# Row maxima of attention scores: two maxima per VectorE instruction, with cells and PSUM banks ordered for it

## The reference, cut to what matters

```python
xn = layer_norm(x, norm_w, norm_b)
q = (xn @ q_w + q_b).reshape(Bx, Tx, H, -1)
k = (xn @ k_w + k_b).reshape(Bx, Tx, H, -1)
att = jnp.einsum('bnhl,bmhl->bnmh', q, k)
att = att + (1.0 - mask) * -1000000.0
att = jax.nn.softmax(att, axis=2)
v = ((xn @ v_w + v_b) * src_mask[:, :, None]).reshape(Bx, Tx, H, -1)
y = jnp.einsum('bnmh,bmhl->bnhl', att, v).reshape(Bx, Tx, Dx)
...
h = layer_norm(y, sb_norm_w, sb_norm_b) * (1.0 + scale) + shift
h = jax.nn.silu(h) @ out_w + out_b
return x + h
```

## Time and profile before

| | us |
|---|---|
| median of three runs | 611.57 |
| lowest and highest | 608.18, 619.8 |
| the profiled execution's own time | 609.58 |
| its span in the trace | 607.4 |
| PE busy in it | 560.7 (92%) |
| DVE busy | 447.2 (74%) |
| ACT busy | 337.8 (56%) |
| POOL busy | 104.3 (17%) |

### The profile page before, as it was taken

How to read it: one execution, slowest core, us unless ns; L and a number is a source line. 1 busy time by engine, 2 the same in 40 slices (tenths; PEclk the granted TensorE clock), 3 DMA queues, 4 the chain that set the end, 5 groups by cost and what they waited for, 6 DMA issues and landing times. The chain is left out here.

```text
span 607.4 us, 8411 instructions
## 1 busy us (share of the span) xinstructions
PE 560.7 (92%) x3060; PEld 274.5 (45%) x3060; DVE 447.2 (74%) x896; ACT 337.8 (56%) x411; POOL 104.3 (17%) x171
## 2 busy tenths in 40 slices
PE   8998996999999899999989999999889999987976
PEld 8554432434533343453334345455335443524765
DVE  6488674878688989887988988769888886314552
ACT  1533473555587666448667565765585566662530
POOL 4098506000000402000020230000422020002200
PEclk9999897999999999999999999999899999999998
DMA  4243985556201040404031010010002100000002
GB/s 131 80 128 74 184 273 160 140 131 143 66 27 29 2 82 0 83 1 81 25 58 28 1 28 0 6 55 19 12 2 62 35 3 2 1 0 1 1 2 69
DMA packets 18580, 33.74 MB, mean 56 GB/s; under 512 B 3930, under 2 KB 10450, under 8 KB 17772
## 3 DMA queue, kind: packets, MB, share of 16 engines
q1 hardware_dynamic: 18430, 33.18, 22.2%
q10 hardware_dynamic: 110, 0.03, 0.0%
HBM read 19.29 MB, written 13.52 MB: 54 GB/s over the span
## 5 line engine op out<-in xcount | busy, mean ns | idle before, releaser
L867 ACT ACTIVATE prob<-sT 128x1024 f32<-128x1024 f32 x256 | 247.8, 1023 | 122.0 <-PE sT L1043 121.7
L1222 DVE TENSOR_REDUCE halfmax<-bank 128x1 f32<-128x512 f32 x424 | 269.3, 684 | 60.3 <-PE bank L928 58.5
L928 PE MATMUL bank<-ks,qs 50*128 50x512 f32 x424 | 152.0, 476 | 15.2 <-DVE halfmax L1222 8.2
L1063 PE MATMUL bank<-prob,vp 128*17 128x512 f32 x1024 | 136.4, 605 | 0.6 <-ACT prob L867 0.6
L928 PEld LDWEIGHTS bank<-ks,qs 50*128 50x128 f32 x424 | 62.3, 184 | 124.9 <-DVE halfmax L1222 71.8
L1043 PE MATMUL sT<-qs,ks 52*128 52x512 f32 x512 | 105.8, 426 | 10.6 <-DMA qs<-crows 6.5
L652 POOL TENSOR_TENSOR rstd<-var,neghalf 128x4 f32<-128x4 f32 x12 | 12.2, 1015 | 430.8 <-DVE var L1146 430.8
L1043 PEld LDWEIGHTS sT<-qs,ks 52*128 52x128 f32 x512 | 53.2, 187 | 28.0 <-ACT prob L867 11.4
L1222 DVE TENSOR_REDUCE halfmax<-sT 128x1 f32<-128x512 f32 x88 | 56.8, 685 | 8.5 <-PE sT L928 7.4
L903 PE MATMUL bank<-w,hT 128*128 128x256 f32 x152 | 38.7, 388 | 1.2 <-ACT hT L789 1.2
L1063 PEld LDWEIGHTS bank<-prob,vp 128*17 128x17 f32 x1024 | 17.0, 95 | 40.4 <-issue 37.6
(11 more groups left out here) (178 smaller groups left out, 561.5 us busy)
## 6 DMA issues: line engine op xcount, KB each, us to landing
stack_rows<-late SPq DMA_DIRECT2D x12, 512.0 KB, 6.7
qs<-stack_rows SPq DMA_DIRECT2D x30, 192.0 KB, 3.4
ks<-stack_rows SPq DMA_DIRECT2D x14, 384.0 KB
stack_rows<-late SPq DMA_DIRECT2D x17, 256.0 KB, 5.0
out_x<-xs SPq DMA_DIRECT2D x4, 512.0 KB, 2.9
xs<-in_x SPq DMA_DIRECT2D x4, 256.0 KB, 3.8
xs<-in_x SPq DMA_DIRECT2D x2, 512.0 KB, 4.3
late<-in_L_cond_emb_w SPq DMA_DIRECT2D x1, 1024.0 KB, 9.2
```

The costliest lines, as they stand in the source:

```text
L867: act.activation(prob[:, c % 2, 2 * u:2 * u + 2, :].rearrange("p j n -> p (j n)"), sT[u][:, :], ACT.Exp).then_inc(exp_done, 1)
L928: last = pe.matmul(o, qs[rows, s % SLOTS, c, t * P:(t + 1) * P], ks[rows, hg, c, half * HALF:(half + 1) * HALF], start=True, stop=True)
L1063: last = pe.matmul(acc[32 * j:32 * j + VW, :], vp[:, b, c, hg * GH + j, :], prob[:, c % 2, 2 * u + two, :], start=(c == 0), stop=(c == NT ...
L1222: dve.tensor_reduce(halfmax[:, s % 2, r, half:half + 1], o, axis=AX.X, op=ALU.max, negate=True).then_inc(u.done, 1)
```

## The change

`cell` is ordered anew for subproblems 1 to 15, so that product m+1 differs from an even m only in the head of a pair, and `halfmax` is laid out so that product m's result has the place m. The three ring banks become one PSUM tensor, `ring3`. `follower` names the successor of each product in the same group and subproblem. `place` gives a product and its follower two neighbouring banks at once where the two banks that come free first are neighbours (`at_once`), in which case no third product is paired with them; where they are not, it sometimes passes over the middle bank of the ring (number 1) and takes the one that comes free second. Two lent products are a pair as well. VectorE then waits for the second product of a pair, takes both maxima with one instruction (128 x 2 results from 128 x 1024 numbers) at the first one's place in its order, and counts its semaphore up by 2; a TensorE fill that waits for either bank waits for that instruction. The 32nd maximum's joining instruction reads `halfmax` with other strides.

```diff
--- before.py
+++ after.py
@@ -122,7 +122,7 @@
         shift = sb("shift", [P, LAYERS, QT])
         neghalf = sb("neghalf", [P, QT])
         unused = sb("unused", [P, 1])
-        halfmax = sb("halfmax", [P, 2, GH * QT, NH])
+        halfmax = sb("halfmax", [P, 2, MAXES])
         negmax = sb("negmax", [P, 2, GH * QT])
         cpieces = sb("cpieces", [P, 2, 2, PARTS, GH * QT // 2])
         crows = sb("crows", [2 * PARTS * GH * QT // 2, 2, P])
@@ -170,8 +170,10 @@
         select = qs[0:PARTS, 1, 0, 0:P]
 
         sT = [ctx.enter_context(nc.psum_tensor(f"sT{i}", [P, 2 * HALF], F32)) for i in range(2)]
-        single = [ctx.enter_context(nc.psum_tensor(f"bank{i}", [P, HALF], F32)) for i in range(4, 8)]
-        B8 = [sT[i // 2][:, (i % 2) * HALF:(i % 2 + 1) * HALF] for i in range(4)] + [t[:, :] for t in single]
+        single = ctx.enter_context(nc.psum_tensor("bank4", [P, HALF], F32))
+        ring3 = ctx.enter_context(nc.psum_tensor("bank5", [P, 3 * HALF], F32))
+        B8 = [sT[i // 2][:, (i % 2) * HALF:(i % 2 + 1) * HALF] for i in range(4)] + [single[:, :]]
+        B8 += [ring3[:, i * HALF:(i + 1) * HALF] for i in range(3)]
         acc = B8[4]
 
         def bend(h):
@@ -412,17 +414,36 @@
         dve_end += [("y1", b, 0), ("y1", b, 1)] + norm[:-1] + [("y1", b, 2)] + norm[-1:] + [("y1", b, 3)] + dve_layer("mid1", 1)
         dve_end += [("out1", b, s) for s in range(4)]
 
+
+
+        follower, at_once = {}, {}
+        for runs_of_step in runs + [[ahead[:2], ahead[2:5], ahead[5:]]]:
+            for run in runs_of_step:
+                follower.update({one: other for one, other in zip(run, run[1:]) if one[1] == other[1] > 0})
+
         unit = {}
+        bank_of = {}
 
         def place(order, banks, ready, on_act, on_dve, done_act, done_dve, taken=None):
 
 
             nth = {key: i + 1 for seq in (on_act, on_dve) for i, key in enumerate(seq)}
             held = [None] * len(banks)
+            chosen = {}
             for i, key in enumerate(order):
                 j = i % len(banks)
-                if taken is not None:
-                    j = min(range(len(banks)), key=lambda x: -len(order) if held[x] is None else taken[held[x]])
+                if key in chosen:
+                    j = chosen[key]
+                elif taken is not None:
+                    oldest = sorted(range(len(banks)), key=lambda x: -len(order) if held[x] is None else taken[held[x]])
+                    j = oldest[0]
+                    if key in follower and i + 1 < len(order) and order[i + 1] == follower[key] and abs(oldest[0] - oldest[1]) == 1:
+                        j = min(oldest[:2])
+                        chosen[follower[key]] = j + 1
+                        at_once[key] = follower[key]
+                    elif j == 1 and held[1] is not None and taken[held[oldest[1]]] <= taken[held[1]] + 4:
+                        j = oldest[1]
+                bank_of[key] = j
                 former, held[j] = held[j], key
                 unit[key] = Unit(banks[j], ready, i + 1, done_act if key[0] in ON_ACT else done_dve, nth[key], unit.get(former))
 
@@ -449,15 +470,20 @@
             lent += maxima(k, 3)
             lent_after.append(len(lent))
             for j, key in enumerate(maxima(k, 3)):
+                bank_of[key] = j
+                if j == 0 and key in follower:
+                    at_once[key] = follower[key]
                 unit[key] = Unit(B8[j], lent_ready, lent.index(key) + 1, lent_done, lent.index(key) + 1, None)
         place(end_order, B8[0:7], end_ready, [key for key in act_end if key in end_order], [key for key in dve_end if key in end_order], end_act, end_dve)
 
+        second = set(at_once.values())
+
         def cell(s, m):
 
 
             if s == 0:
                 return m // 16, m % 2, m // 2 % QT, m // 8 % 2
-            return m // 4 % 2, m % 2, m // 8, m // 2 % 2
+            return m // 16, m % 2, m // 4 % QT, m // 2 % 2
 
         def where(k):
             s, c = divmod(k, NT)
@@ -1212,17 +1238,25 @@
                     dve.wait_ge(kexp_ready, (b + 1) * KC)
                     dve.reciprocal(rksum[:, b, :], ksum[:, b, :]).then_inc(rk_ready, 1)
                     return
+                if kind == "max" and key in second:
+                    return
+                first, key = key, at_once.get(key, key)
                 u = unit[key]
                 o = u.bank
                 dve.wait_ge(u.ready, u.ready_at)
                 if kind == "max":
                     s, m = key[1:]
                     c, two, t, half = cell(s, m)
-                    r = (two * 2 + c) * QT + t
-                    dve.tensor_reduce(halfmax[:, s % 2, r, half:half + 1], o, axis=AX.X, op=ALU.max, negate=True).then_inc(u.done, 1)
+                    position = (c * QT + t) * 4 + 2 * half + two
+                    if first != key:
+                        pair = (sT[0] if u.ready is lent_ready else ring3)[:, bank_of[first] * HALF:(bank_of[first] + 2) * HALF]
+                        dve.tensor_reduce(halfmax[:, s % 2, position - 1:position + 1], pair.rearrange("p (j n) -> p j n", j=2), axis=AX.X, op=ALU.max, negate=True).then_inc(u.done, 2)
+                    else:
+                        dve.tensor_reduce(halfmax[:, s % 2, position:position + 1], o, axis=AX.X, op=ALU.max, negate=True).then_inc(u.done, 1)
                     if m == MAXES - 1:
                         dve.wait_ge(u.done, u.done_at)
-                        dve.tensor_reduce(negmax[:, s % 2, :], halfmax[:, s % 2, :, :], axis=AX.X, op=ALU.min).then_inc(csplit, 1)
+                        dve.tensor_reduce(negmax[:, s % 2, :].rearrange("p (two r) -> p two r", two=2),
+                                          halfmax[:, s % 2, :].rearrange("p (r h two) -> p two r h", h=NH, two=2), axis=AX.X, op=ALU.min).then_inc(csplit, 1)
                         dve.wait_ge(csplit, 2 * s + 1)
                         both = negmax[:, s % 2, :].rearrange("p (two c) -> p two c", two=2)
                         dve.tensor_copy(cpieces[:, s % 2, :, 0, :].bitcast(F32R), both).then_inc(csplit, 1)
```

## The result

The change is slower. Medians: 644.03 us against 613.12, ratio 1.0297 (95% interval 1.0224 to 1.037). Measured again as one of the experiments, on one chip with 17 runs of the kernel before: 645.78 against 610.79, ratio 1.0498 (1.0429 to 1.0568). The changed kernel's times spread from 624 to 651 us, and go with TensorE's mean granted clock, run by run. One run of 1661.85 us at clock 1.00 stands alone; nothing here explains it.

The account below looks back on a forecast made before the run. TensorE's order of work was taken as the bound, VectorE close behind. Terms 4.9 + 2.7 + 2.7 + 0.8 + 0.5 - 2.0 = +9.6 us on 609.58 gave 619.2; predicted 619, range 606 to 628.

Parts of the forecast that it names:

- (a): Eleven steps 3, 1, 1, 0: the fill between scores and values waits for a pair; 4.9 us, bounds 2.7 and 5.9.
- (b): Steps 37, 45, 69, 77 and 100: the second transpose waits for the pair before it; 2.7 us, lower bound 0.
- (c): Nine steps: a second filler takes the bank of the single product just made; 2.7 us, bounds 0.9 and 3.9.
- (d): Step 107: its first product waits for the addition of `out1`; 0.8 us.
- (e): Step 102: `neg` waits for the pair 0+1 while VectorE is behind; 0.5 us.
- gain of 30 pairs: Steps 3, 1, 1, 0 and neighbours, where VectorE runs without a gap: saved instruction starts of some 30 pairs, -2.0 us.
- The cover that the forecast gave steps 0 to 6: Delays in steps 0 to 6 cost nothing while TensorE afterwards waits 4.9 us for a DMA; otherwise about 1 us.
- Rival C: TensorE's clock falls more often, behind the six runs of steps 3, 1, 1, 0; four falls give 626 us; chance 0.13.
- A: VectorE sets the pace, in steps 3, 1, 1, 0 and those with large fillers: faster, 598.8 or 584.7 us; chance 0.10.
- the 0.065: VectorE: us saved per pair read by one instruction in a series, 10.8 us for 166 pairs.
- B: All effects of the change lie beside other work: 608 to 612 us; chance 0.15.
- D: Every `neg` is late, not only step 102's, its bank being a pair's: twelve more at 0.54, 625.7 us; chance 0.12.

Follow-up runs that it names:

- e8_lent_only: Kernel before with the new order of cells and one instruction for each of the 42 pairs in lent banks, ring as before: 612.11 us, ratio 1.001.
- e5_no_middle_rule: Changed kernel without the rule that keeps single products out of the middle bank, 139 pairs instead of 166: 626.05 us, ratio 1.0276 to the kernel before.
- e1_singles: Changed kernel with its order of cells and banks, but VectorE takes every maximum by itself: 637.02 us, ratio 1.0425 to the kernel before.
- e2_wait: Kernel before, but in eleven steps the fill between scores and values waits for one maximum more: 619.78 us, ratio 1.0154.
- e9_middle_rule_alone: Kernel before with the new order of cells and only the middle-bank rule, no pair taken at once: 638.04 us, ratio 1.0409.

## Why the prediction was wrong

Forecast: +9.6 us over the profiled 609.58, range to 628. The medians are 644.03 and 645.78. Two steps of the sum failed: the rule about the middle bank was priced only where a filler meets it (2.7 us, where it cost at least 7), and the clock was taken as unchanged (it cost about 12). The repeat's profile has nearly the clock of the former's (0.974 and 0.982) and a span 19.4 us longer: 626.8 against 607.4. Where they lie:

| term | forecast | repeat |
|---|---|---|
| (a) eleven steps 3, 1, 1, 0 | +4.9 | 34: 0.16, 35: 0.29, 36: 0.52, 44: 0.53, 60: 0.62, 61: 0.38, 66: 0.17, 67: 0.28, 68: 0.53, 101: 0; 76 by the first profile 0.53; 4.0 |
| (b) transposes behind a pair | +2.7 | 37: 0.64, 45: 0.55, 69: 0.63, 100: 0.64; 77 by the first profile 0.57; 3.0 |
| (c) second filler behind a single product | +2.7 | 9: 0.41, 54: 0.37, 86: 0.37, 89: 0.48, 99: 0.22, 105: 0.42, 115: 0.26; 85: 0.10; 88: 0; 2.6 |
| (d) steps 106, 107 | +0.8 | 0.83 - 0.15 = 0.7 |
| (e) step 102 | +0.5 | 0.70 |
| gain of 30 pairs | -2.0 | not to be told apart; `e8_lent_only` shows none for 42 pairs |
| prologue | none | +4.6 |
| steps 76, 77 at half clock | none | (1.00 - 0.53) + (1.62 - 0.57) = +1.5 |
| the rest: steps 0 to 8 (step 7 is 3.1 shorter), 13 to 17, 81, 98, 103, 108 | 0 | 19.4 + 0.6 (first maximum 0.6 earlier) - 11.0 - 4.6 - 1.5 = +2.9 |

*The sum.* The five terms came to 11.0 us, where 11.6 was forecast, or 9.6 with the gain. So the priced waits came at nearly their price. Three things failed:

- **The search for places.** Term (c) asked only where a filler meets the rule that avoids the middle bank. The rule stands in `place` for the whole ring, prologue and first subproblem too, where there are no pairs to pay for it. It cost 4.6 us there. (c), (d) and (e) are gone without it (`e5_no_middle_rule`). The choice of banks has a part in the rest too: steps 13 to 17 and 81 grow in `e1_singles`, without pairs, by 1.2 and 0.6. A line of the diff that I had priced at 2.7 us cost at least 7. The cover that the forecast gave steps 0 to 6, a wait of 4.9 us for a DMA, was 2.7 in the first profile, and the delay of the prologue came through all the same.
- **What a wait was put down to.** Term (a) gave the 0.54 to the pair's late bank. The number was right, in part by luck: in seven of the eleven steps `e1_singles` has the later predecessor with no pair, and in step 60 the same wait (1.34 us, against 1.27), since rule and choice of banks together put the fill on m 23. (e) is of the same kind: `neg` of step 102 stands on m 1, not on m 0, and the step grows in `e1_singles` too (0.87, part of it at half clock). In steps 34 to 36 and 76, and in (b) for 37, 77 and 100, it was the pair, as forecast. Which to blame matters: taking out only the instruction would have saved 3 us at an equal clock, taking out only the rule 10.
- **The clock.** The sum took TensorE's clock as it was. Rival C had the mechanism and the places (behind the runs of 3, 1, 1, 0 and their neighbours), and a wrong price: four falls of 4.0 us at 1.7 us each, 6.9, from the one short fall in the earlier trace rows. They lasted 13.7, 20.5 and 23.9 us. In the first profile 24.1 of the 34.5 us by which the steps grew lie in the 20 steps touched by half clock there or before. Over all 11 runs the mean clock is 0.943, against 0.972: 2.9 x 4.2 = 12 us beside the 17.5 at an equal clock. A chance of 0.13 was too little, since the waits of (a) and (b) lay in just such stretches.

*The other rivals.* A (VectorE paces) is out: `e8_lent_only` saved 42 starts for nothing, and VectorE waited more, not less, for products (0.72 us instead of 0.20 for m 26 in step 60). VectorE's busy time fell by 5.9 us, to 441.3, not to 436. Its durations add up to 23.3 us less (495.1 and 471.8), but where one instruction's end overlaps the next one's start the time counts once, and 17.4 us of such overlap went with them. Two single maxima in a row and the next start 1.20 us apart, a pair and the next 1.13, as the 0.065 had it. By my estimate from the formula of the Trainium skill ("VectorE: DVE Perf Modes", TRN2 errata) a pair would save 157 ns; in a series it saved 70 here, and in `e8_lent_only` none of it is seen at the end. B (all hidden) is out. D (every `neg` late) did not come: step 62 grew by 0.08 us in the first profile.

On C, the Trainium skill ("TensorE: Matmul & The Clock Gate", psum-queue depth-cycling) has short idle times between banks lower the clock again and again. `e2_wait` agrees (0.972 to 0.955 for eleven waits); `e9_middle_rule_alone` does not bear it out: 24 us lost at an equal clock, not 2.6, and 0.970 against 0.976.

*Still open.* Which of the waits bring the clock down, and why the fall lies in other steps in each run; why rule and instruction together (627) cost less than `e9_middle_rule_alone` (634): that run has other predecessors (262 units, 167 of them read later), so it shows that the rule costs by itself and does not measure its price inside the change.

## What to carry to other kernels

Where a few PSUM banks go round between TensorE and VectorE, the currency is when each bank comes free, not VectorE's instruction count: list for every fill whose bank it takes and when that one is read, before and after, over the whole program. 150 fills moved to a later predecessor were most of the loss at an equal clock (14 of 17.5 us, `e1_singles`); 11 cost nothing clear of the scatter until a longer instruction held the first bank. A rule that reserves a bank must be limited to the places that use it. A sign that you name for a cause is worth as much as the time: `e9_middle_rule_alone` was slow as expected and had its waits elsewhere. And where TensorE is 94% busy, price its clock too: here the added waits cost 17.5 us and the clock about 12 more.

## What the runs showed of the hardware

- One VectorE maximum over two PSUM banks takes 1.222 us (166 times), as long as a reduction over 1024 numbers from SBUF (1.220); two over one bank take 0.685 each and start 0.60 apart. Reading two banks in one instruction shows no price of its own, and both banks come free at its end: the load waits until 1.27 us after its start.
- Eleven waits of some 0.6 us were enough to take TensorE's mean granted clock from 0.972 to 0.955 and the median up by 11 us, at an equal clock by 2.6 (`e2_wait`, four runs).
- The same program's mean clock ranges from 0.925 to 0.977 between runs of the change and 0.946 to 0.986 between runs of the kernel before; 0.01 is worth 4.2 us of some 610.
- The first row maximum of the same changed kernel starts at 20.7 us in one profile and at 24.1 in the other: 3.4 us by chance of the run, which a single profile can't tell from an effect.
